# Shared-key attention: the early exponentials taken head by head from PSUM with a bias

## What is computed

```python
q = _rmsnorm(_rope(q), q_norm_w)
k = _rmsnorm(_rope(k), k_norm_w)
scores = jnp.einsum('bqgtd,bqgsd->bqgts', q, k) * scale
scores = jnp.where(mask[None, None, None], scores, NEG)
attn = jax.nn.softmax(scores, axis=-1)
out = jnp.einsum('bqgts,bqgsd->bqgtd', attn, v)
```

## Time and profile before

| | us |
|---|---|
| median of 3 runs | 3449.14 |
| lowest and highest run | 3446.36, 3449.71 |
| the profiled execution, its time | 3445.07 |
| the profiled execution, its span | 3443.3 |

### The profile page before, as it was taken

One profiled execution on the slowest core, in us unless ns is written; L12 is line 12 of the kernel. 1 busy time (PEld: TensorE's weight loads), 2 busy tenths in 40 slices (PEclk: granted clock), 3 DMA queues, 4 the chain that ended last, 5 costly groups with the idle time before them and its releaser, 6 DMA issues. The chain is left out here.

```text
span 3443.3 us, 62072 instructions
## 1 busy us (share of the span) xinstructions
PE 3109.0 (90%) x22971; PEld 1935.4 (56%) x22971; DVE 2146.6 (62%) x4177; ACT 1801.2 (52%) x3979; POOL 1169.1 (34%) x1166
## 2 busy tenths in 40 slices
PE   5999979999999999998988879997699999988999
PEld 5999856446464646436754543333456666665444
DVE  5999735015353535336847744445699999974777
ACT  1323235665656564755644533334466666664666
POOL 3666511001010101105716612224477777760000
PEclk9999989999999999999999989999799999998999
DMA  2000000000000000000000022220100000003676
GB/s 85 15 19 11 1 18 12 1 8 1 6 1 6 1 6 1 6 7 2 2 8 1 1 57 56 57 56 16 24 10 5 4 5 5 4 1 44 72 68 65
DMA packets 75395, 66.43 MB, mean 19 GB/s; under 512 B 20374, under 2 KB 70584, under 8 KB 74680
## 3 DMA queue, kind: packets, MB, share of 16 engines
q1 hardware_dynamic: 75096, 62.45, 10.6%
HBM read 55.58 MB, written 2.51 MB: 17 GB/s over the span
## 5 line engine op out<-in xcount | busy, mean ns | idle before, releaser
L707 ACT ACTIVATE p_hidden<-p_hid_ps,net_bias 128x344 f32<-128x344 f32 x816 | 382.6, 549 | 227.7 <-PE p_hid_ps L654 169.3
L2447 POOL TENSOR_TENSOR p_qt<-p_qt,p_q_sum 97x512 f32<-97x512 f32 (+1 forms) x44 | 46.4, 1055 | 731.9 <-DVE p_q_sum L2401 731.9
L680 PE MATMUL p_y_ps<-p_hidden,net_down 128*64 128x344 f32 x1632 | 285.7, 466 | 2.1 <-DVE p_hidden L756 2.1
L654 PE MATMUL p_hid_ps<-xn,net_up 64*128 64x344 f32 x1248 | 241.4, 488 | 8.2 <-PEq L316 4.6
L2759 DVE TENSOR_TENSOR p_hid<-p_silu,p_pair_ps 128x344 f32<-128x344 f32 x288 | 134.9, 508 | 173.1 <-PE p_pair_ps L2708 94.1
L756 DVE TENSOR_TENSOR p_hidden<-p_hidden,p_row 128x344 f32<-128x344 f32 x384 | 175.6, 514 | 76.0 <-ACT p_hidden L707 47.5
L2740 ACT ACTIVATE p_silu<-p_pair_ps 128x344 f32<-128x344 f32 x288 | 116.0, 454 | 201.6 <-PE p_pair_ps L2697 201.6
L1919 POOL TENSOR_TENSOR p_rot<-p_rot,p_cross 128x512 f32<-128x512 f32 x128 | 160.5, 1278 | 126.6 <-DVE p_cross L2074 126.6
L680 PEld LDWEIGHTS p_y_ps<-p_hidden,net_down 128*64 128x64 f32 x1632 | 103.1, 136 | 158.8 <-issue 49.1
L1932 POOL TENSOR_TENSOR p_prob<-p_prob,p_total 128x1024 f32<-128x1024 f32 (+1 forms) x128 | 185.6, 1471 | 12.4 <-DVE p_total L2100 12.4
L654 PEld LDWEIGHTS p_hid_ps<-xn,net_up 64*128 64x128 f32 x1248 | 106.0, 189 | 128.4 <-ACT p_hidden L707 77.8
(11 more groups left out here) (457 smaller groups left out, 8055.6 us busy)
## 6 DMA issues: line engine op xcount, KB each, us to landing
p_row<-gated_rows SPq DMA_DIRECT2D x192, 86.0 KB, 2.9
p_row<-mark_rows SPq DMA_DIRECT2D x192, 86.0 KB, 10.0
p_x<-in_tok_x SPq DMA_DIRECT2D x16, 384.0 KB, 3.1
out<-h SPq DMA_DIRECT2D x12, 172.0 KB, 2.9
shared_value_pairs<-shared_values SPq DMA_DIRECT2D x16, 128.0 KB, 2.5
p_swapped<-xn SPq DMA_DIRECT2D x64, 32.0 KB, 1.9
p_kinds<-in_tok_c3w SPq DMA_DIRECT2D x1, 1280.0 KB, 9.7
thirds_fold<-in_L_fold SPq DMA_DIRECT2D x1, 1156.5 KB, 5.2
```

What stands on the lines that cost most here:

```text
L654: mm = pe.matmul(hid_ps[k % ring][:, 0:TILE], w_up[half(g), n, :], x[half(g), cols(t)], start=True, stop=not experts or by_rows)
L680: mm = pe.matmul(y_ps[u][half(g), 0:TILE], w_down[:, n, :], hid[k % hidden_ring][:], start=n == 0, stop=last and not experts)
L707: act.activation(hid[k % hidden_ring][:], hid_ps[k % ring][:, 0:TILE], func, bias=b_up[:, n:n + 1]).then_inc(act_done.sem, 1)
```

## The change

In the early half VectorE no longer subtracts. It multiplies the maxima by minus the scale into a small new buffer `below` (128x8), and ScalarE takes the exponential of each of the 8 head pairs (128x64) from PSUM, with its column of `below` as bias, and writes `prob`. `lowered` is now counted up by the small multiplication. As ScalarE now reads the early scores in PSUM, `score(n)` waits for the exponentials of round n-1 too. The late half is as before.

```diff
+        below = [ph.sb(f"below{r}", [P, MS]) for r in two]
...
                     if n:
                         pe.wait_ge(lowered.sem, lowered.at(2 * n))
+                        pe.wait_ge(exped.sem, exped.at(2 * n))
...
                 def exponentials(n, ty):
                     act.wait_ge(lowered.sem, lowered.at(2 * n + 2 - ty))
                     p = prob[n % ring_p][ty]
-                    act.activation(p[:], p[:], ACT.Exp, scale=D ** -0.5).then_inc(exped.sem, 1)
+                    if ty == LATE:
+                        act.activation(p[:], p[:], ACT.Exp, scale=D ** -0.5).then_inc(exped.sem, 1)
+                        return
+                    if n >= ring_p:
+                        round_made(("early", n - ring_p))
+                    for m in range(MS):
+                        ins = act.activation(p[:, m, :], scores[EARLY][:, m, :], ACT.Exp, scale=D ** -0.5,
+                                             bias=below[n % 2][:, m:m + 1])
+                    ins.then_inc(exped.sem, 1)
...
                     dve.wait_ge(topped.sem, topped.at(k))
+                    if ty == EARLY:
+                        if n >= 2:
+                            dve.wait_ge(exped.sem, exped.at(2 * (n - 1)))
+                        dve.tensor_scalar(below[n % 2][:], stat[n % 2][:, ty, :], -(D ** -0.5), None,
+                                          ALU.mult).then_inc(lowered.sem, 1)
+                        return
                     if n >= ring_p:
-                        wait_made(("late1" if ty == LATE else "early", n - ring_p))
-                    wide = HALF_SEQ * (1 + ty)
+                        wait_made(("late1", n - ring_p))
+                    wide = P
```

## The result

| | before | after |
|---|---|---|
| median of 4 runs, us | 3447.75 | 3632.94 |
| profiled span, us | 3443.3 | 3631.6 |
| mean granted clock | 0.969 | 0.950 |

The changed kernel takes 1.0536 times as long (95% interval 1.0518 to 1.0555), 185 us more. The forecast was 165 us more, in a range of 107 to 211.

The account below looks back on a forecast made before the run. The prediction took the chain of TensorE and ScalarE from score to score as the bound. The wait's 119 us plus the clock's 46 us gave +165 us, a forecast of 3614 us, with a range of 3556 to 3660 us.

Parts of the forecast that it names:

- What bounds the kernel: In the 64 rounds, all of a round hangs on score's start through TensorE and ScalarE; VectorE's work lies beside that chain.
- (a): VectorE's early subtraction becomes a 128x8 multiplication: 0.49 us a round saved, worth nothing on the path.
- (b): ScalarE's early exponential becomes eight of 128x64 with a bias: 1.76 us instead of 0.64.
- (c): TensorE's score waits for the previous round's early exponentials: mean 1.99 us per ordinary round, 119 us in all.
- (d): TensorE's clock halves after some pauses: 28 stretches at 1.65 us each, 46 us, bounds 0 and 74.
- one ordinary round in two: Assumed share of ordinary rounds whose TensorE pause is followed by half clock: 28 stretches.
- What I looked for: Signs in the trace: score's waits in 63 rounds, exponential lengths, round lengths, VectorE's share, and the stage's granted clock.
- VectorE as the bound: Rival: VectorE's 93% is the limit, each round loses 0.49 us, 3418 us; chance 0.03.
- a hidden wait: Rival: score's new wait is met when TensorE arrives and changes nothing, 3449 us; chance 0.03.
- Clock holds: Rival: TensorE's clock does not fall, only the wait's 119 us is added, 3568 us; chance 0.28.
- the second rival: Clock falls in most rounds (3642 us), or the eight exponentials don't overlap (3662 us); chance 0.15.

Follow-up runs that it names:

- wait_only: Kernel before plus only score's new wait for the early exponentials; subtraction and single exponential stay; 3495.63 us, ratio 1.0152.
- early_first: Changed kernel with early maxima first, eight exponentials right after the first copy of the queries, score waiting for those of the round before; 3459.84 us, ratio 1.0035.
- q1_first_change: early_first with `below` written with a step of two elements and `copy_out` behind the second copy of the queries; 3447.53 us, ratio 1.0004.
- eight_sbuf: Changed kernel without score's new wait: VectorE copies early scores to SBUF, ScalarE takes the eight biased exponentials there; 3495.53 us, ratio 1.0152.
- fill4: Changed kernel with four unused matmuls of 512 columns in front of TensorE's new wait; 3565.68 us, ratio 1.0348.

## Why the prediction was right, and where it was off

- **What bounds the kernel** (the chain of TensorE and ScalarE from score to score): right. wait_only lengthened that chain at its end and cost 53 us; early_first took all of the new work out of the end and cost 12.
- **(a) VectorE's saving is worth nothing on the path**: right. Its size, 0.49 us, was too large. The reciprocal of 128x8 that stood for the multiplication was no guide: the multiplication took 0.27 us in the mean of the changed kernel (0.17 in the median), but 0.57 in q1_first_change (median 0.79), where VectorE is full and the saving would have counted. There 0.12 us a round is left of it.
- **(b) eight exponentials in 1.76 us**: 1.75 measured. Each one was longer than estimated (0.35 for 0.315 us) and the pitch a little shorter, (1.75 - 0.35)/7 = 0.200 us. The 2.0 us estimated from the Trainium skill (ScalarE: Activation LUTs, What ACT_TABLE_LOAD costs) fit the eight from SBUF, 2.01 us in eight_sbuf; from PSUM it was the row that held.
- **(c) the wait, 119 us**: 123 by fill4. Score starts 1.90 us after the first exponential begins, not 1.81, so the signal is 0.15 us instead of 0.05, a figure for which the prediction named no row. Of the 2.07 us a round (11.40 - 9.31 and 12.21 - 10.16), 0.08 vanish when the pause is filled.
- **(d) the clock, 46 us**: the mechanism was right and its size was not. The price of a stretch was 1.58 us for the 1.65 predicted; their number was 40 for the 28 of "one ordinary round in two". 40 x 1.58 = 63 us; the changed kernel against fill4 gives 62 to 67. The ten pauses of the kernel before, six of them followed by a fall, would have given 0.6 x 55 = 33; I rounded that down to a half without a row for it. The other seven stretches no row of the kernel before could tell, and why the clock fell behind 39 of 55 nearly equal pauses and not behind the other 16 stays open. The rule of the Trainium skill (TensorE: Matmul & The Clock Gate, Why this matters for your kernels), by which the clock would hold, is not borne out here: at 39 of 55 pauses of 2.0 us, shorter than the gap it allows, the clock fell.
- **What I looked for**: waits at `score` in 63 rounds, yes, about 2 us each and 123 us in all; exponentials of 0.35 us where 0.315 was named; rounds of 11.3 and 12.1, yes (11.40, 12.21, and 1.6 more with a fall); VectorE at 73%, measured 67%, and the stage's clock of 0.94, measured 0.90, both off because the clock fell more often.
- **The rivals**: neither VectorE as the bound nor a hidden wait. "Clock holds" would have been right with a filled pause. The clock's part of the second rival, that it falls in most rounds, is what came: 40 stretches lie nearer to its 45 than to the forecast's 28, and 3633 us nearer to its 3642 than to 3614. So the direction, the wait and the chain were foreseen; that the time lies inside the range is owed to a range drawn wide enough to take in a rival given 0.15.

119 + 46 = 165 predicted; 123 + 62 = 185 measured.

## What to carry to other kernels

When an engine starts to read a single-buffered PSUM bank directly, ask what stood between that read and the next write to the bank, and where the reader comes in its own queue. Here the reader was the last step of a round and the writer the first of the next, so work that used to be free came to lie between two scores, and saving 0.5 us on a 93% busy engine was worth nothing. The same instructions 4 us earlier before the next score cost a fifteenth of it.

A pause on TensorE can cost more than its length. Price it twice: its own time, and the matmuls behind it at half clock if the clock falls. Here the pauses of 2.0 us cost about half as much again as the wait itself (62 on 123 us); those of 0.9 us in wait_only brought no fall. Taking the pause away, as early_first does, gained 173 us; where it can't be taken away, a few unused matmuls in it are worth trying, which gained some 60.

## What was not expected of the hardware

- TensorE's clock fell to 1.2 GHz (0.50) at 39 of 55 pauses of 2.0 us and at one of 7 of 1.10 us (the changed kernel), and at none of the pauses of 0.9 to 1.0 us in wait_only and fill4. With four unused matmuls in the pause it stayed at 2.4 GHz, which gave about 62 us back.
- A VectorE multiplication of 128x8 took from 0.17 to 1.5 us; each of the 458 that took over 0.25 us ended 24 to 32 ns behind the end of a GpSimd instruction.
- Eight biased exponentials of 128x64 took 1.75 us from PSUM and 2.01 us from SBUF.
